# A Swin block: token blocks of paired 7x7 tiles, moved in 11 pieces in place of 5

## What is computed

```python
xn = layernorm(x, ln1_w, ln1_b)
xs = jnp.roll(xn, shift=(-SHIFT, -SHIFT), axis=(1, 2))            # SHIFT = 3
xw = xs.reshape(B, H // WS, WS, W // WS, WS, C)                   # WS = 7
xw = xw.transpose(0, 1, 3, 2, 4, 5).reshape(-1, N, C)             # N = 49 tokens of one 7x7 tile
q, k, v = split(xw @ qkv_w + qkv_b)                               # 6 heads of 32
attn = softmax(einsum('bhqd,bhkd->bhqk', q, k) * scale)
o = einsum('bhqk,bhkd->bhqd', attn, v)                            # then @ proj_w + proj_b, tiles and roll undone
x = shortcut + o
h = gelu(layernorm(x, ln2_w, ln2_b) @ mlp_w1 + mlp_b1, approximate=False)
x = x + (h @ mlp_w2 + mlp_b2)
```

## Time and profile before

| | us |
|---|---|
| median of 3 runs | 2984.17 |
| lowest and highest | 2982.33 and 2984.73 |
| the profiled execution's own time | 2986.28 |
| its span, first to last instruction | 2984.1 |

### The profile page before, as it was taken

How to read it: one execution, slowest core, us unless ns; L and a number is a source line. 1 busy time by engine, 2 the same in 40 slices (tenths; PEclk the granted TensorE clock), 3 DMA queues, 4 the chain that set the end, 5 groups by cost and what they waited for, 6 DMA issues and landing times.

```text
span 2984.1 us, 116983 instructions
## 1 busy us (share of the span) xinstructions
PE 2935.4 (98%) x43446; PEld 2865.3 (96%) x43446; DVE 2680.2 (90%) x6816; ACT 2266.7 (76%) x4472; POOL 1435.0 (48%) x1678
## 2 busy tenths in 40 slices
PE   5999999999999999999999999999999999999997
PEld 5999999999999999999999999999999999999997
DVE  5899999999999999999999999999999999999986
ACT  3778777777777777787777777777777877777774
POOL 2445444454544445454444545444454544445443
PEclk7999999999999999999999999999999999999999
DMA  1010010011001001100100110010011001000100
GB/s 47 25 29 24 24 31 26 24 27 29 24 24 30 26 24 27 29 24 24 31 26 24 27 29 24 24 30 26 24 27 29 24 24 30 26 24 27 30 21 18
DMA packets 109318, 79.68 MB, mean 27 GB/s; under 512 B 7294, under 2 KB 108782, under 8 KB 109294
## 3 DMA queue, kind: packets, MB, share of 16 engines
q1 hardware_dynamic: 108740, 78.56, 9.8%
q10 hardware_dynamic: 554, 0.79, 0.1%
HBM read 40.78 MB, written 38.54 MB: 27 GB/s over the span
## 4 chain that ended last, share of the span: by engine, by line
PE 97%; DVE 1%; issue 1%; DMA 1%; ACT 0%; POOL 0%; ACTq 0%; SPq 0%; DVEq 0%; POOLq 0%
PE ps L941 35%; PE ps L944 16%; PE ps L1053 5%; PE ps L972 5%; PE ps L1014 5%; PE ps L1026 5%; PE ps L1073 5%; PE ps L1027 5%; PE ps L1016 5%; PE ps L1015 5%; PE ps L903 3%; PE ps L911 2%; PE ps L1034 2%; PE ps L1038 1%; PE ps L913 1%
## 5 line engine op out<-in xcount | busy, mean ns | idle before, releaser
L426 POOL TENSOR_TENSOR gl<-g,gh 128x392 fp32r<-128x392 f32 x512 | 567.9, 1133 | 289.2 <-ACT gh L786 279.8
L941 PE MATMUL ps<-zh,w 128*128 128x392 f32 x3072 | 698.0, 342 | 0.6 <-ACT zh L738 0.6
L941 PEld LDWEIGHTS ps<-zh,w 128*128 128x128 f32 x3072 | 550.1, 188 | 0.8 <-ACT zh L738 0.8
L297 POOL TENSOR_TENSOR prob<-prob,rcp 128x588 f32<-128x588 f32 x128 | 152.2, 1189 | 746.2 <-DVE rcp L638 746.2
L780 ACT ACTIVATE g<-ps,biasf 128x392 f32<-128x392 f32 x768 | 397.4, 594 | 130.2 <-PE ps L941 130.2
L941 PE MATMUL ps<-zh1c,wqkv 128*128 128x392 f32 x1536 | 363.2, 345 | 11.0 <-DVE zh1c L488 11.0
L418 POOL CAST zh<-zh1c 128x392 fp32r<-128x392 f32 x256 | 134.0, 524 | 451.0 <-DVE z L478 434.6
L786 ACT ACTIVATE gh<-g 128x392 fp32r<-128x392 f32 x756 | 350.1, 552 | 0.0
L752 ACT ACTIVATE oh<-ps 128x392 fp32r<-128x392 f32 (+1 forms) x256 | 118.9, 521 | 279.1 <-PE ps L1073 279.1
L622 DVE TENSOR_TENSOR gl<-g,gh 128x392 fp32r<-128x392 f32 x256 | 289.8, 1170 | 5.7 <-ACT gh L786 5.7
L941 PEld LDWEIGHTS ps<-zh1c,wqkv 128*128 128x128 f32 x1536 | 281.1, 191 | 13.1 <-issue 11.6
(11 more groups left out here) (112 smaller groups left out, 7488.1 us busy)
## 6 DMA issues: line engine op xcount, KB each, us to landing
xin<-in_x SPq DMA_DIRECT2D x128, 147.0 KB
out<-yo SPq DMA_DIRECT2D x128, 147.0 KB
xin<-in_x SPq DMA_DIRECT2D x128, 71.2 KB
out<-yo SPq DMA_DIRECT2D x128, 71.2 KB
xin<-in_x SPq DMA_DIRECT2D x128, 54.8 KB
out<-yo SPq DMA_DIRECT2D x128, 54.8 KB
xin<-in_x SPq DMA_DIRECT2D x128, 18.8 KB
out<-yo SPq DMA_DIRECT2D x128, 18.8 KB
```

Source lines behind the costliest of these rows:

```text
L426: pool.tensor_tensor(gl[:, m, :], g[:, m, :], gh[:, m, :].bitcast(F32), ALU.subtract)\
L941: last = pe.matmul(dst, cols(w, part), act_, start=(n == 0), stop=(n == 4))
```

## The change

1. Block p is now a pair of neighbouring tiles: 7 rows of 14 pixels. `moves` walks over the 7 pixel rows: a piece is 14 partitions (one row of a tile pair) by 4 blocks; where the roll turns the row of the last block, it is cut in 11 and 3. That makes 11 pieces for a load and 11 for a store.
2. `z1` takes the layout of `z2`, and `apply1` writes it in 6 instructions in place of 4 (`in_pairs`, now shared with `apply2`).
3. `transposes1` has 6 transposes, with `by_window`, a permutation of the 98 tokens of a block, in place of the identity; so tokens reach PSUM tile by tile. `in_rows` and `in_windows` go. The narrow high and low parts of norm 1 are made by 2 instructions each, in place of 1, and `zh1_done` counts 3 for each group.
4. The attention output (`pv`) is written 49 columns in a row, in place of 7 by 7; the two tiles of a pair are still joined by `by_window_parity`.
5. `qk` takes tiles 2 and 1 together: passes 0 and 1 of both, which need only the wide high part, then passes 2 to 4 of each; tile 0 comes by itself. Each pass waits only for the parts that it reads.

```diff
+RUN = 2 * WS
-MOVES = 5
+MOVES = WS + 4
...
+        by_window = sb("by_window", [PART, PART])
...
-        z1 = sb("z1", [PART, BLOCKS, C])
+        z1 = sb("z1", [PART, BLOCKS // 2, 2 * C])
...
-            turn = (WS - SHIFT) * SIDE - SHIFT
-            for lo, hi, src in ((0, turn, top + SHIFT), (turn, M - SHIFT, low), (M - SHIFT, M, top)):
-                while lo < hi:
...
+            last = (BLOCKS - 1) * RUN
+            for row, rows, here, there in ((0, WS - SHIFT, top, low), (WS - SHIFT, SHIFT, low, top)):
+                for r in range(rows):
+                    p, at = RUN * (row + r), here + SHIFT + r * SIDE
+                    whole = BLOCKS - (r == rows - 1)
+                    yield p, RUN, slice(0, whole), at * C, [[C, RUN], [RUN * C, whole], [1, C]]
+                yield p, RUN - SHIFT, slice(BLOCKS - 1, BLOCKS), (at + last) * C, [[C, RUN - SHIFT], [1, C]]
+                yield p + RUN - SHIFT, SHIFT, slice(BLOCKS - 1, BLOCKS), there * C, [[C, SHIFT], [1, C]]
...
+            pool.tensor_copy(by_window[:, :].rearrange("p (w r c) -> p w r c", w=2, c=WS),
+                             ident[0:PART, 0:PART].rearrange("p (r w c) -> p w r c", w=2, c=WS)).then_inc(ident_ready, 1)
...
             def low_parts1(grp):
 
-                wait(dve, zh1_done, 2, grp, 1)
-                dve.tensor_tensor(in_windows(zl1c[:, :]), in_rows(ps[:, T1, 0:M]), in_windows(zh1c[:, 0, :]).bitcast(F32),
-                                  ALU.subtract).then_inc(zl1_done, 1)
-                wait(dve, zh1_done, 2, grp, 2)
-                dve.tensor_tensor(in_windows(zh1c[0:64, 1, :]), in_rows(ps[64:128, T1 + 1, 0:M]),
-                                  in_windows(zh1c[64:128, 1, :]).bitcast(F32), ALU.subtract).then_inc(zl1_done, 1)
+                wait(dve, zh1_done, 3, grp, 1)
+                dve.tensor_tensor(zl1c[:, :], ps[:, T1, 0:M], zh1c[:, 0, :].bitcast(F32), ALU.subtract).then_inc(zl1_done, 1)
+                for odd in range(2):
+                    hi, lo = slice(64 * odd, 64 * odd + 64), slice(64 - 64 * odd, 128 - 64 * odd)
+                    wait(dve, zh1_done, 3, grp, 2 + odd)
+                    last = dve.tensor_tensor(blocks_of(zh1c[lo, 1, :], odd), stacked(ps[hi, T1 + 1, 0:M // 2]),
+                                             blocks_of(zh1c[hi, 1, :], odd).bitcast(F32), ALU.subtract)
+                last.then_inc(zl1_done, 1)
...
             def apply1(grp, parity):
                 wait(dve, t1_done, 1, grp - 1, 1)
-                pieces = [(z1[:, p, :], p, slice(0, C)) for p in range(BLOCKS)]
-                norm_apply(xin[:, parity, :, :], mv1, rs1, pieces, grp, mv1_done, rs1_done, z1_done)
+                norm_apply(xin[:, parity, :, :], mv1, rs1, in_pairs(z1), grp, mv1_done, rs1_done, z1_done)
...
             def transposes1():
 
                 for p in range(BLOCKS):
-                    for part in range(2):
-                        last = pe.transpose(ps[:, T1 + part, span(p)], z1[:, p, 64 * part:64 * part + 128],
-                                            ident[0:PART, 0:PART])
+                    a0 = (C + B) * (p % 2)
+                    pe.transpose(ps[:, T1, span(p)], z1[:, p // 2, a0:a0 + A], by_window[:, :])
+                for h in range(BLOCKS // 2):
+                    last = pe.transpose(ps[:, T1 + 1, span(h)], z1[:, h, A:A + 2 * B], by_window[:, :])
                 last.then_inc(t1_done, 1)
...
-                wait(pe, zh1_done, 2, i, 2)
-                wait(pe, zl1_done, 2, i, 2)
                 for t in tiles:
-                    project(ps[:, QK[t], 0:M], zh1c, zl1c, wqkv, lambda w, part: w[:, part, 128 * t:128 * t + 128])\
+                    tile(t, (0, 1), {0: [(zh1_done, 3, i, 1)]})
+                for t in tiles:
+                    tile(t, (2, 3, 4), {2: [(zl1_done, 2, i, 1)], 3: [(zh1_done, 3, i, 3), (zl1_done, 2, i, 2)]})\
                         .then_inc(qk_done, 1)
...
-                                    dst = ps[cols, PV + w, h // 4 * M // 2:(h // 4 + 1) * M // 2]\
-                                        .rearrange("p (r q c) -> p q r c", q=PAIRS, c=WS)[:, p]
+                                    dst = ps[cols, PV + w, h // 4 * M // 2 + TOK * p:h // 4 * M // 2 + TOK * (p + 1)]
...
-                    qk(i + 1, (2,))
-                    qk(i + 1, (1, 0))
+                    qk(i + 1, (2, 1))
+                    qk(i + 1, (0,))
```

## The result

The changed kernel takes 3005.68 us (median of 4 runs, 3004.49 to 3008.91) against 2984.45 before: ratio 1.0074, 95% interval 1.0062 to 1.0086. It is slower by 21 us, as forecast in sign, but the forecast was 118 us slower, and the cause that it named isn't the cause.

A forecast was written before the change was run, and what follows sets the result against it. PE, 97% of the chain, bound the kernel; the change would make SP's store-and-load loop bind at 23.65 us a group. 2986.3 + 113 + 5 gives 3104, taken as 3102 us; range 2980 to 3200.

The forecast's parts named there:

- the sum as a loop: SP's store and load plus DVE's statistics to `yo`: 23.65 us a group, 0.92 over the period, +113 us over 123 bodies.
- The circle: SP can't load before it has stored, DVE can't make `yo` before the load's statistics; 23.65 us, against 19.5 before.
- the gap: On SP, from the last store piece to the first load piece: 1.0 us, the mean of 0.80 and 1.20.
- landing: From the last load piece's start until its data is there: 1.7 us taken, 4.1 the upper bound.
- In the steady part PE waits for nobody: Read from the profile's waits: PE waited three times for DVE's low parts, all at the start.
- two distances: DVE's second `gl` ends 0.96 us before PE reads it; the narrow low part ends 0.24 before `qk`.
- PE: 0.14 a body: Two of 8 norm 1 transposes go: 0.14 us a group, 18 us in all, if PE stays the bound.
- a circle of 22.8 to 23.15: Case of a smaller store-and-load loop than forecast: time 2990 to 3040 us, chance 0.05.
- A: Rival: the load still lands in time and PE gives back its 0.14 us; 2971 us, chance 0.12.
- The signs of being wrong: In the new profile: no wait for `xin` with PE at 97%, pieces not 0.56 apart, or PE waiting within `qk`.
- The new order of q and k: In `qk` on PE: leaves 0.45 us for the narrow low part, late by 0.45 with the old order.
- Start and end: Six more pieces ahead of the first parameter rows and six behind the last `yo`: 5.9 less about one, +5 us.

The follow-up runs named there:

- the better order of PE: Changed kernel with norm 1's six transposes put between the two halves of the softmax transposes on PE: 2947.39 us, ratio 0.9876 to the kernel before.

## Why the prediction was wrong, step by step

Two steps failed: the sum as a loop, which gave the forecast's +113 us, and the list of what PE waits for, which left out the wait that gave the measured +21.

- **The sum as a loop (23.65 us), the term that was to decide.** The circle exists, and binds with the slow piece among the last. In the changed kernel it doesn't: with each load ahead of the store the time is the same. Its terms, predicted and measured in the changed kernel (means of the two parities): DVE from the statistics to `yo` without its waits for PE 9.29 and 8.8; the step to the store 0.46 and 0.45; the store from first to last start 5.6 and 5.3; the gap 1.0 and 1.0; the load 5.6 and 5.35; landing 1.7 and 1509.74 - (1503.08 + 5.37) = 1.3. In all 22.2 us in place of 23.65, under the period of 22.91 and under the 22.44 of the version with the better order of PE. The transfers were sized too long by 0.95 together, and DVE's way by 0.5. DVE's term I had taken as fixed, but its two `gl` took 2.34 us in the kernel before, 1.77 in the changed one, and 1.01 where DVE came late.
- **"In the steady part PE waits for nobody", and two distances.** The reading of the waits was right, the list of distances wasn't complete. PE has a third meeting with DVE, `x2_done` ahead of the second half of the softmax transposes, and it had no room. `apply1` was costed at +0.39 and that was right (1.62 against 1.24), but I followed it only to the `gl` and the low parts, behind `stats1`, and not to the first thing behind it, the residual. Measured by itself this costs 47 us. DVE's waits of 0.39 and 0.41 us a body for PE didn't help, as I said of the other places: they lie ahead of the work.
- **PE: 0.14 a body.** Measured 0.17 (0.62 to 0.45). With 0.38 lost by `apply1` and 0.17 gained a body is 0.21 us longer, 26 us over 124 bodies. The pieces added 5.5, which makes 31 against 21 measured. By the spans of the profiled executions it is nearer: +43.8 for `apply1` alone, +2.5 for the pieces alone and +20.1 for all, so the rest of the change gave back 26.2, 0.21 a body. That agrees with the 0.22 measured on the better order of PE; 0.04 to 0.05 of it isn't assigned.
- **Landing.** The bounds, 0.8 and 4.1, held in the changed kernel. The 2.0 us that the Trainium skill gives a transfer as fixed cost (DMA: Bandwidth & Descriptors, Anatomy of one DMA), there for transfers that GpSimd issues, lies above the 1.3 measured here from the start of SP's last issue. With the 73-token piece among the last four it was 1522.24 - (1512.62 + 5.51 - 0.26) = 4.4, near the 4.1 that I had put on a load with that piece; that agrees with the same page's rule (Why a DMA increments its semaphore by 16 and not by 1) on how many engines share a transfer.
- **The range and the rivals.** 2980 to 3200 holds the time, and so does the case of a circle of 22.8 to 23.15 (2990 to 3040, at 0.05), but by its number alone: the period came to 22.91 through PE's wait for the residual, and no rival had that. A's condition came true, since the load lands in time; its 2971 didn't, since PE lost more than it gave back. I wrote that condition as 0.05 less for each piece "or 0.45 a piece", which aren't the same: 0.56 less 0.05 is 0.51, and the pieces came out at 0.52 to 0.54. The range held by luck.
- **The signs of being wrong.** DVE's wait for `xin` was to be 150 to 200 us and was 30.5; its waits for the scores and the turned result were to go and stand as before (0.36 and 0.41). PE's wait was to be within `qk` and stands at the softmax transposes.
- **The new order of q and k:** costed as cover for 0.45 us. In the changed kernel it covers nothing, with the wait removed it is worth 0.34.
- **Start and end:** I had +5. The traces of the changed kernel and of the kernel before have the first `yo` at 97.57 and 97.64 us, and 5.6 and 6.3 us behind the last, so nothing is lost at either end.

## What to carry to other kernels

When an instruction gets longer, follow its engine's list from there on, and for each signal that goes out compare its time with that of the first instruction that needs it; start with the very next one, and don't stop at those that look tight. A distance of 0.1 us between two engines that a trace shows as no wait at all can already be used up: PE started 0.15 us behind the end of the residual that it waited for. And where a VectorE or GpSimd instruction on SBUF tiles takes longer in the trace than its smallest value, look whether the two engines overlap there. Such a duration can move when anything moves: don't put it into a sum as a constant.

## What the runs showed of the hardware

- Work of DVE on SBUF tiles takes longer beside GpSimd's: six `tensor_scalar` of 98 partitions took 3.78 us beside GpSimd's three `tensor_tensor`, and 1.62 with those cut to 8 columns; a DVE `tensor_tensor` with two SBUF inputs took 554 to 1170 ns in the mean. The Trainium skill (SBUF — State Buffer, Who interferes with whom) has both forms: VectorE's second port pair is shared with GpSimd; `tensor_scalar` can enter a two-port mode, in which whoever comes first holds the shared one for the whole instruction, and a `tensor_tensor` with two SBUF inputs contends with GpSimd instructions that read SBUF. The durations agree; which port was held no trace here shows. The prediction left this out because the change adds no GpSimd work, but the 2.34 us of the earlier trace rows already held it.
- A transfer's issue on SP, with its address instructions, comes every 0.52 to 0.54 us in the mean over a row of 11 (5.21 / 10 in a store, 5.37 / 10 in a load), with pieces of 3 to 56 rows.
- The idle time shown on PE's matmuls isn't what a wait costs: it was 0.25 us on the matmuls and 0.44 on the weight loads ahead of them, while from start to start 0.45 was lost against the order without the wait.
